# A graph layer's edge sum: a list's base is made behind a unit's second step, the product with it and the ranks one step later

## The chip, the cores and the metric

The kernel runs on one core of a Trainium2 chip. The metric is the device time of one execution in microseconds (us), lower is better. The kernel before has a median of 2552.46 us over 3 runs (2551.87 to 2553.11).

## What is computed

One layer of a graph network on 6250 nodes with 256 features, in float32. 200,000 edges, sorted by their target, carry a source, a target and a weight.

```python
xn = _layernorm(x, axis=-1)
gathered = values[:, None] * x[col]                    # one row per edge
out = jax.ops.segment_sum(gathered, row, num_segments=OUT_FEATURES) + bias
x = x + out_of_edges(xn, edge_index, edge_weight, node_vec1) + linear_attention(xn)
x = x + mixture_of_8_experts(_layernorm(x, axis=-1), top_k=2)
```

The change touches only the sum over the edges (the `gathered` and `segment_sum` lines above).

## The kernel before, in words

The program has five parts in a row: constants, `front` (layer norm, keys and values, loading the edges), `edge_sum`, `stragglers`, and the routing and the experts. All of the change is in `edge_sum`, which is written out without loops: four functions, one for each of TensorE (`tensor`), ScalarE (`scalar`), VectorE (`vector`) and GpSimd (`gpsimd`), each with its own instruction order, held together by semaphores.

The nodes are cut into 49 tiles of 128. The edges of a target tile are a list of 128 x 34 places. Each list is **sorted** by source tile (a *sort*, number `s`), so that later each (source tile, target tile) pair can be handled by small products. Independently the 49 x 7 pairs of target tile and group of seven source tiles are **summed**. Both kinds of work are interleaved by hand in `schedule`: eight sorts come first (`AHEAD`), then 7 groups of 7 *units*; a unit is 7 *steps*, one target tile each, so there are 343 steps. In the first six groups (42 units) each unit also does one sort, cut into pieces that hang behind its steps (`if more and i == 0:` and so on, where `i` is the step, 0 to 6; "the second step" is `i == 1`). The last group (7 units) has no sorts, but the second layer norm and the transposes for the routing.

A step of the sum, the same in each of the 343:

- VectorE: `picks` (L1295), `hots` (one-hot matrices: L1284, L1288) and `add` (L1316, adds a finished tile from PSUM to the sum in SBUF). `picks` runs one step ahead of TensorE's use, `hots` two, `add` one behind it.
- TensorE: `blocks` of the next tile (12 products, L903, waits for L1288), then `rows` of this one (4 products L911, 3 products L915; waits for ScalarE's copy and for the add of the tile two before).
- ScalarE: `evacuate` (L1027, copies the block matrices that L903 made).
- GpSimd: three gathers of rows from memory (L817).

The pieces of a sort in the order of the data: ScalarE repeats the list's tile numbers (`repeat_tiles`, L973) and fields (`repeat_fields`, L981); VectorE compares (`hot_tiles`, L1121); TensorE makes the **base** (`base`, L845: 34 products of 49 columns, which count for each partition how many edges of the same tile lie before it); ScalarE copies the base from PSUM (`take_base`, L989); VectorE multiplies it with the comparison (`rank_ahead`, L1134), compares within a row (`in_row`, L1125) and adds up the **ranks** (`rank`, L1140, L1142, L1145); ScalarE repeats the ranks (`repeat_ranks`, L996); VectorE makes `values` (L1164, four in all: two, one and one) and `slots` (L1153); TensorE makes the **table** from these (`make_table`, L854: 34 products of 196 columns); ScalarE unpacks it, and VectorE finishes it with `part` (L1172, L1173; in four of the seven units of a group) or `make_list` (L1180 to L1186; in the others).

Where the pieces stood before: step 0: TensorE `base` behind the rows, ScalarE unpacking, `take_base`, a repeat of the fields, VectorE the first two `values`; step 1: VectorE `part`, `in_row`, `rank_ahead`, ScalarE a repeat; step 2: VectorE `rank`; step 3: VectorE `make_list`, one of `values`; step 4: the last of `values`, ScalarE `repeat_ranks`; step 5: `slots`; step 6: `hot_tiles` for the next sort, TensorE `make_table`. Buffers of the sort are single: `values` may only be written again when the table that reads them is made (`table_made`).

Of the kernel before, what the change touches and what calls it, by code (L numbers as in the profile page):

```python
# [615 lines left out]
def edge_sum(nc, shared, edges, mixing, hot_w, xn_dram, xT_dram, base_dram, sum_dram, z_dram, Wg, bg, bias, wg, gb_row, G, NG, NT, N, D, HD):  # L616
# [22 lines left out]
    with ExitStack() as ctx:  # L639
# [86 lines left out]
        def later(s):  # L726

            return not (isinstance(s, int) and s == 0)
# [92 lines left out]
        def _(pe):  # L821
# [101 lines left out]
            def unit(g, k, odd, par, turn, more, after, q):  # L923
                t = g * NT + k * BU
                s = g * GRP + k + AHEAD
                pe.wait_ge(window_in[par], 16 * (turn + 1))
                for i in range(BU):
                    if i + 1 < BU:
                        blocks(t + i + 1, (i + 1) % 4, (odd + i + 1) % 2)
                    elif after:  # L930
                        blocks(t + BU, 0, 1 - odd)
                    rows(t + i, i, g * GRP + k, (odd + i) % 2, par)
                    if not more:
                        n = k * BU + i - BU - 1
                        if n >= 0:
                            turn_z(n)
                        if n >= 1:
                            logits(n - 1)
                    if more and i == 0:
                        base(s)  # L940
                    if more and i == 6:
                        make_table(s)
# [11 lines left out]
        def _(act):  # L954
# [29 lines left out]
            def take_base(s):  # L984

                if later(s):
                    act.wait_ge(ahead_done, 3 * s)
                act.wait_ge(base_done, s + 1)
                act.copy(base_sb[:, :], base_ps).then_inc(base_in, 1)  # L989
# [59 lines left out]
            def unit(g, k, odd, par, turn, more, after, q):  # L1049
                u = g * GRP + k  # L1050
                t = g * NT + k * BU
                s = u + AHEAD
                turned = isinstance(k, int) and k == GRP - 1
                for i in range(BU):
                    if i + 1 < BU:
                        evacuate(t + i + 1, (odd + i + 1) % 2)
                    elif after:
                        evacuate(t + BU, 1 - odd)
                    if not more:
                        if k > 0 and i == 0:  # L1060
                            root(k - 1)
                        if k * BU + i > BU:
                            take_z(k * BU + i - BU - 1)
                    if more and i == 0:
                        if odd == par:
                            unpack(s - 1, q, 1 - par)
                        else:
                            unpack_list(s - 1, lists_before(g + 1, q), q, 1 - par)
                        take_base(s)
                        repeat_fields(s, 2, 3)  # L1070
                    if more and i == 1:
                        repeat_fields(s, 3, FIELDS)
                    if after and i in (2, 4):
                        if turned:
                            act.wait_ge(unpacked, (g + 2) * GRP)
                            act.wait_ge(parted, (g + 2) * DENSE)
                            act.wait_ge(listed, (g + 2) * 3 * PICK)
                            take(t, 1 - odd, 1 - par, 0, i // 2 - 1)
                        else:
                            take(t, 1 - odd, par, k + 1, i // 2 - 1)  # L1080
                    if more and i == 3:
                        repeat_fields(s + 1, 0, 1)
                    if more and i == 4:
                        repeat_ranks(s)
                    if more and i == 5:
                        repeat_tiles(s + 1)
                    if more and i == 6:
                        repeat_fields(s + 1, 1, 2)
# [12 lines left out]
        def _(dve):  # L1101
# [206 lines left out]
            def unit(g, k, odd, par, turn, more, after, q):  # L1308
                u = g * GRP + k
                s = u + AHEAD  # L1310
                t = g * NT + k * BU

                def add(i):
                    row = acc[:, bass.ds(k * BU + i, 1), 0:D].rearrange("p a d -> p (a d)")
                    dve.wait_ge(o_done, t + i + 3)
                    dve.tensor_tensor(row, row, sum_ps[(odd + i) % 2], ALU.add).then_inc(o_added, 1)  # L1316

                    if not more:
                        dve.wait_ge(o_added, t + i + 3)
                        statistics(k * BU + i)  # L1320

                for i in range(BU):
                    if i + 1 < BU:
                        picks(t + i + 1, i + 1, odd)
                    elif after:
                        picks(t + BU, 0, 1 - odd)
                    if i == 2:
                        dve.wait_ge(cur_done, 2 * (u + 1))
                    if i + 2 < BU:
                        hots(t + i + 2, i + 2, odd, t + i + 2 if i + 2 < 3 else t + i + 1)  # L1330
                    elif after:
                        if i == BU - 2:
                            dve.wait_ge(cur_done, 2 * (u + 1) + 1)
                        hots(t + i + 2, i + 2 - BU, 1 - odd, t + i + 2)
                    if i > 0:
                        add(i - 1)
                    if not more and k > 0:
                        if i == 1:
                            reciprocals(k - 1)
                            normalize((k - 1) * BU)  # L1340
                        if i > 0:
                            normalize((k - 1) * BU + i)
                    if more and i == 0:
                        values(s, 0, 2)
                    if more and i == 1:
                        if odd == par:
                            part(s - 1, q, 1 - par)
                        in_row(s)
                        rank_ahead(s)
                    if more and i == 2:  # L1350
                        rank(s)
                    if more and i == 3:
                        if odd != par:
                            make_list(s - 1, lists_before(g + 1, q), q, 1 - par)
                        values(s, 2, 3)
                    if more and i == 4:
                        values(s, 3, FIELDS)
                    if more and i == 5:
                        slots(s)
                    if more and i == 6:  # L1360
                        hot_tiles(s + 1)
                add(BU - 1)
                if not more:
                    merge(k)
# [751 lines left out]
```

## Time and profile before, and how to read it

| what | value |
|---|---|
| median of 3 runs | 2552.46 us |
| span of the profiled execution, first to last instruction | 2536.7 us |
| its own time | not listed beside the span; the median is 15.8 us above the span |
| TensorE matmul busy | 2230.1 us, 88% of the span |
| VectorE busy | 1963.9 us, 77% |
| GpSimd busy | 1551.1 us, 61% |
| ScalarE busy | 1174.3 us, 46% |

PE is TensorE's matmuls, PEld its weight loads, DVE is VectorE, ACT ScalarE, POOL GpSimd. A number in brackets behind a row is the time that the engine sat idle before it, with what ended it: another engine's instruction, "issue" (nothing that the profile shows), or "remote" (a semaphore whose raiser the profile could not place near). The ends of matmuls are modelled, so a signal of PE is best read from when the engine that waits for it starts.

### The profile page before, as it was taken

How to read it: one execution, taken by the hardware profiler on the slowest of the kernel's cores; microseconds unless marked ns; L12 is line 12 of the kernel's file. 1: busy time of each engine (PE TensorE's matmuls, PEld its weight loads, DVE VectorE, ACT ScalarE, POOL GpSimd, SP SyncE). 2: the span in 40 equal slices, each digit the busy share in tenths (PEclk: the TensorE clock that was granted, in tenths of full speed). 3: DMA queues.
4: the chain of work that ended last, by engine and by line, in shares of the span. 5: the costliest groups of instructions: out<-in, count | busy, mean ns of one | idle time of the engine just before them, and what ended most of it. 6: DMA issues, size and time to landing. Idle time of an engine off the chain costs nothing. (4 is left out here: it accounts for less than half of the span.)

```text
span 2536.7 us, 45539 instructions
## 1 busy us (share of the span) xinstructions
PE 2230.1 (88%) x16549; PEld 1930.5 (76%) x16550; DVE 1963.9 (77%) x3350; ACT 1174.3 (46%) x1696; POOL 1551.1 (61%) x1356
## 2 busy tenths in 40 slices
PE   7987799999999899989988998999989944999993
PEld 4656687777887788778877787778877844999993
DVE  7989888788898788878877897879877757555552
ACT  2236544443444344434443454444322235888772
POOL 4750266666676566666665666666766612778883
PEclk9989999999999899989988999999999977999997
DMA  5532422222223222222222222222244453455555
GB/s 151 150 113 87 123 82 75 76 90 78 74 83 90 73 82 76 88 76 80 76 82 73 83 79 84 78 79 77 82 123 139 136 180 61 79 81 83 82 81 133
DMA packets 160931, 235.90 MB, mean 93 GB/s; under 512 B 54834, under 2 KB 121805, under 8 KB 160490
## 3 DMA queue, kind: packets, MB, share of 16 engines
q0 software_dynamic: 70896, 164.43, 25.4%
q1 hardware_dynamic: 75536, 55.29, 7.9%
q10 hardware_dynamic: 14314, 13.68, 1.6%
q8 instruction: 120, 1.97, 0.3%
q14 instruction: 65, 0.53, 0.1%
HBM read 186.46 MB, written 53.24 MB: 94 GB/s over the span
## 5 line engine op out<-in xcount | busy, mean ns | idle before, releaser
L817 POOL DMA_INDIRECT picked<-xn_dram,place x1029 | 1143.9, 1112 | 721.7 <-PE bank L915 289.8
L1027 ACT COPY stage<-bank 128x512 f32<-128x512 f32 x343 | 201.0, 586 | 796.9 <-remote 477.6
L915 PE MATMUL bank<-picked,pick_w 128*128 128x256 f32 x2058 | 518.4, 389 | 3.3 <-issue 3.3
L915 PEld LDWEIGHTS bank<-picked,pick_w 128*128 128x128 f32 x2058 | 405.7, 197 | 65.8 <-issue 5.2
L911 PE MATMUL bank<-window,stage 128*128 128x256 f32 x1568 | 416.9, 409 | 17.8 <-issue 12.8
L903 PE MATMUL bank<-hot_w,hots 128*128 128x128 bf16 x4116 | 312.0, 225 | 49.1 <-issue 44.8
L911 PEld LDWEIGHTS bank<-window,stage 128*128 128x128 f32 x1568 | 300.4, 202 | 65.1 <-issue 25.6
L1164 DVE TENSOR_TENSOR vals<-hot_t,field_rep 128x1666 bf16<-128x1666 bf16 x200 | 203.7, 1041 | 187.8 <-remote 180.2
L1288 DVE TENSOR_TENSOR hot_w<-hots,cur 128x1536 bf16<-128x1536 bf16 x343 | 328.6, 958 | 11.9
L903 PEld LDWEIGHTS bank<-hot_w,hots 128*128 128x128 bf16 x4116 | 267.1, 101 | 92.5 <-issue 54.5
L911 PE MATMUL bank<-stage 128*128 128x256 f32 x1176 | 315.5, 410 | 11.6 <-issue 10.4
L981 ACT COPY field_rep<-fields 128x1666 bf16<-128x1666 bf16 (+1 forms) x193 | 322.8, 1677 | 1.2 <-DVE vals L1164 1.2
L1284 DVE TENSOR_TENSOR hots<-ends,cur 128x1408 bf16<-128x1408 bf16 x343 | 303.1, 884 | 1.7 <-ACT cur L1021 1.7
L911 PEld LDWEIGHTS bank<-stage 128*128 128x128 f32 x1176 | 225.9, 203 | 49.0 <-issue 23.2
L1908 POOL DMA_INDIRECT sum_dram<-y,target x112 | 179.1, 1599 | 64.0 <-issue 31.1
L1316 DVE TENSOR_TENSOR acc<-acc,bank 128x256 f32<-128x256 f32 x343 | 142.3, 415 | 85.2 <-PE bank L915 44.7
L1295 DVE TENSOR_TENSOR pick_w<-hots,cur_w 128x384 f32<-128x384 bf16 x343 | 190.6, 556 | 0.2
L1899 POOL DMA_INDIRECT zin<-z_dram,token x112 | 115.5, 1031 | 83.4 <-POOLq L1600 49.6
L2002 PE MATMUL bank<-w,hh 128*128 x896 | 163.6, 282 | 1.1 <-DVE hl L2050 1.1
L854 PE MATMUL bank<-vals,slot 128*128 128x196 bf16 x1700 | 155.8, 249 | 4.9 <-issue 4.0
L854 PEld LDWEIGHTS bank<-vals,slot 128*128 128x128 bf16 x1700 | 147.9, 98 | 12.3 <-issue 5.8
L2002 PEld LDWEIGHTS bank<-w,hh 128*128 128x128 f32 x896 | 138.2, 189 | 1.4 <-issue 1.4
(253 smaller groups left out, 3414.6 us busy)
## 6 DMA issues: line engine op xcount, KB each, us to landing
picked<-xn_dram,place POOLq DMA_INDIRECT x1029
w<-in_L_ffn_W_dram SPq DMA_DIRECT2D x16, 512.0 KB, 8.9
xn_dram<-xn ACTq DMA_DIRECT2D x49, 128.0 KB, 1.9
xT_dram<-xT ACTq DMA_DIRECT2D x49, 128.0 KB, 2.1
base_dram<-acc SPq DMA_DIRECT2D x7, 896.0 KB
sum_dram<-acc SPq DMA_DIRECT2D x7, 896.0 KB
z_dram<-vals SPq DMA_DIRECT2D x7, 896.0 KB
out_dram<-sum_dram SPq DMA_DIRECT2D x1, 6250.0 KB, 21.8
```

Of the source, the lines that this page charges most:

```text
L817: pool.indirect_dma_start(out=picked[:, i % SETS * PICK + q, :], out_offset=None, in_=xn_dram, in_offset=bass.IndirectOffsetOnAxis(ap=plac ...
L854: mm = pe.matmul(table_ps, slot[:, c, :], vals[:, c, :, :], start=(c == 0), stop=(c == CH - 1))
L903: mm = pe.matmul(block_ps(pp, j), hot[buf][:, PICK + j, :], hot_w[buf][:, part, j, :], start=(part == 0), stop=(part == 2))
L911: pe.matmul(sum_ps[pp], block_sb[pp][:, j, :], window[par][:, j, :], start=(j == 0), stop=False)
L915: mm = pe.matmul(sum_ps[pp], pick_w[i % SETS][:, q, :], picked[:, i % SETS * PICK + q, :], start=False, stop=(q == PICK - 1))
L981: act.copy(field_rep[:, :, a:b, :], fields[:, a:b, bass.ds(s, 1), :].rearrange("p f a c -> p (a c) f").unsqueeze(3).broadcast_to([P, CH, b ...
L1027: act.copy(block_sb[pp].rearrange("p j c -> p (j c)"), banks[pp][:, :]).then_inc(a_copied, 1)
L1164: ins = dve.tensor_tensor(vals[:, :, f, :], hot_t[:, :, :], field_rep[:, :, f, :], ALU.mult)
L1284: dve.tensor_tensor(to[:, :, :].rearrange("p f (b r) -> p f b r", r=REP), ends[:, :, :].rearrange("p f (b r) -> p f b r", r=REP), of[:, i, ...
L1288: dve.tensor_tensor(hot_w[i % SETS][:, :, :, :].rearrange("p f g (b r) -> p f g b r", r=REP), to[:, AT_SRC:HOTS, :].rearrange("p g (b r) - ...
L1295: dve.tensor_tensor(pick_w[i % SETS][:, :, :].rearrange("p q (b r) -> p q b r", r=REP), hot[i % SETS][:, 0:PICK, :].rearrange("p q (b r) - ...
L2002: mm = pe.matmul(y_ps[i][:, n * D:(n + 1) * D], parts[a][:, c, n * P:(n + 1) * P], w, start=(m == 0), stop=(m == 3 * FC - 1))
```

## The change

Three places of the hand-written order. TensorE makes the base behind the rows of step 1, not of step 0. ScalarE takes it at step 1, behind the last repeat of the fields. VectorE multiplies with it at step 2 (before: step 1), and adds up the ranks at step 3 (before: step 2), ahead of `make_list` and one of `values`. No instruction is added or removed. The eight sorts ahead of the units are not touched.

```diff
@@ TensorE, unit
-                    if more and i == 0:
+                    if more and i == 1:
                         base(s)
@@ ScalarE, unit
                             unpack_list(s - 1, lists_before(g + 1, q), q, 1 - par)
-                        take_base(s)
                         repeat_fields(s, 2, 3)
                     if more and i == 1:
                         repeat_fields(s, 3, FIELDS)
+                        take_base(s)
@@ VectorE, unit
                         in_row(s)
+                    if more and i == 2:
                         rank_ahead(s)
-                    if more and i == 2:
+                    if more and i == 3:
                         rank(s)
-                    if more and i == 3:
                         if odd != par:
                             make_list(s - 1, lists_before(g + 1, q), q, 1 - par)
                         values(s, 2, 3)
```

TensorE around the first unit's base, of before (`bank` is any PSUM bank; L903 is the next tile's blocks, L911 and L915 this tile's rows):

```order
 L915 MATMUL bank<-picked,pick_w 128x256 x3
 L845 MATMUL bank<-hot_t,before 128x49 x34
 L903 MATMUL bank<-hot_w,hots 128x128 x12
 L911 MATMUL bank<-window,stage 128x256 x4
 L915 MATMUL bank<-picked,pick_w 128x256 x3
```

and of the change:

```order
 L903 MATMUL bank<-hot_w,hots 128x128 x12
 L911 MATMUL bank<-window,stage 128x256 x4
 L915 MATMUL bank<-picked,pick_w 128x256 x3
 L845 MATMUL bank<-hot_t,before 128x49 x34
 L903 MATMUL bank<-hot_w,hots 128x128 x12
```

The base has moved past one whole step of the sum (12, 4 and 3 products).

VectorE, steps 1 to 3 of a unit, of before (`earlier` is what `rank_ahead` and `rank` write, `same` what `in_row` writes):

```order
 L1125 TENSOR_TENSOR same<-tile_pad,tile_rep 128x1156
 L1134 TENSOR_TENSOR earlier<-hot_t,base_sb 128x34x49
 L1295 TENSOR_TENSOR pick_w<-hots,cur_w 128x384
 L1284 TENSOR_TENSOR hots<-ends,cur 128x1408
 L1288 TENSOR_TENSOR hot_w<-hots,cur 128x1536
 L1316 TENSOR_TENSOR acc<-acc,bank 128x256
 L1140 TENSOR_TENSOR earlier<-earlier,same 128x34x34
 L1142 TENSOR_TENSOR earlier<-earlier 128x34x24
 L1145 TENSOR_REDUCE rank<-earlier 128x34
```

and of the change:

```order
 L1125 TENSOR_TENSOR same<-tile_pad,tile_rep 128x1156
 L1295 TENSOR_TENSOR pick_w<-hots,cur_w 128x384
 L1284 TENSOR_TENSOR hots<-ends,cur 128x1408
 L1288 TENSOR_TENSOR hot_w<-hots,cur 128x1536
 L1316 TENSOR_TENSOR acc<-acc,bank 128x256
 L1134 TENSOR_TENSOR earlier<-hot_t,base_sb 128x34x49
```

The product with the base now stands behind the next step's add instead of ahead of that step; the three rank instructions follow one step after it. On ScalarE `take_base` (L989) changes places with one repeat (L981) and an evacuation (L1027) and now stands right behind the second repeat.

## Rows read from the trace of the kernel before

**Rows 1.** The page's first line.

```profile
span 2536.7 us, 45539 instructions
```

**Rows 2.** Busy time by stretch: 41 of the 42 units with a sort, then the first without.

```profile
core 0: us, PE busy (x) PEld busy (x) DVE busy (x) ACT busy (x) POOL busy (x), PEclk, DMA share, GB/s
334.00:1803.00 1469.00, 1346.11 (x10252) 1163.16 (x10251) 1218.99 (x1777) 649.14 (x838) 956.18 (x862) 0.93 0.27 80
1803.00:1834.00 31.00, 29.41 (x218) 25.91 (x217) 28.50 (x41) 8.28 (x11) 23.85 (x21) 1.00 0.30 86
```

**Rows 3.** Waits in 334 to 1803: who waited for whom, us, times, longest.

```profile
DVE vals L1164 <- remote: 180.2, 37, 8.3
...
PE bank L845 <- issue: 61.2, 83, 1.2
...
PE bank L903 <- DVE hot_w L1288: 1.1, 1, 1.1
```

**Rows 4.** Timeline of one unit, steps 6 to 3, PE, ACT and DVE: start, us, instruction.

```profile
979.42 3.06 PE L854 MATMUL bank<-vals,slot 128*128 128x196 bf16 x34
...
986.06 0.24 PE L845 MATMUL bank<-hot_t,before 128*128 128x49 bf16 x3
...
987.17 2.00 DVE L1164 TENSOR_TENSOR vals<-hot_t,field_rep 128x1666 bf16<-128x1666 bf16 x2 [4.87 <-remote]
...
989.89 0.99 PE L845 MATMUL bank<-hot_t,before 128*128 128x49 bf16 x22 [1.15 <-issue]
...
991.35 0.41 DVE L1316 TENSOR_TENSOR acc<-acc,bank 128x256 f32<-128x256 f32 x1
991.68 0.77 DVE L1125 TENSOR_TENSOR same<-tile_pad,tile_rep 128x1156 bf16<-128x1156 bf16 x1
...
993.15 0.20 ACT L989 CAST base_sb<-bank 128x49 bf16<-128x49 f32 x1 [2.16 <-remote]
...
993.39 1.05 DVE L1134 TENSOR_TENSOR earlier<-hot_t,base_sb 128x1666 bf16<-128x1666 bf16 x1 [0.93 <-ACT base_sb L989]
994.35 0.55 DVE L1295 TENSOR_TENSOR pick_w<-hots,cur_w 128x384 f32<-128x384 bf16 x1
994.50 1.46 PE L915 MATMUL bank<-picked,pick_w 128*128 128x256 f32 x6
...
995.74 0.96 DVE L1288 TENSOR_TENSOR hot_w<-hots,cur 128x1536 bf16<-128x1536 bf16 x1
...
996.62 0.41 DVE L1316 TENSOR_TENSOR acc<-acc,bank 128x256 f32<-128x256 f32 x1
...
999.35 0.55 DVE L1295 TENSOR_TENSOR pick_w<-hots,cur_w 128x384 f32<-128x384 bf16 x1
```

**Rows 5.** The same unit, its steps 3 to 5: the list and TensorE's need of VectorE.

```profile
1001.94 0.27 DVE L1180 TENSOR_SCALAR table<-table 128x49 uint16<-128x49 uint16 x1
...
1002.63 1.04 DVE L1164 TENSOR_TENSOR vals<-hot_t,field_rep 128x1666 bf16<-128x1666 bf16 x1
...
1004.97 0.96 DVE L1288 TENSOR_TENSOR hot_w<-hots,cur 128x1536 bf16<-128x1536 bf16 x1
...
1007.03 0.83 PE L903 MATMUL bank<-hot_w,hots 128*128 128x128 bf16 x12
```

**Rows 6.** Timeline of an earlier unit: a base without gaps and its copy.

```profile
601.58 1.04 PE L845 MATMUL bank<-hot_t,before 128*128 128x49 bf16 x34
...
602.79 0.20 ACT L989 CAST base_sb<-bank 128x49 bf16<-128x49 f32 x1 [3.10 <-PE bank L845]
```

**Rows 7.** Timeline of the last unit with a sort: end of its base and the copy.

```profile
1782.60 1.12 PE L845 MATMUL bank<-hot_t,before 128*128 128x49 bf16 x23 [1.16 <-issue]
...
1785.93 0.20 ACT L989 CAST base_sb<-bank 128x49 bf16<-128x49 f32 x1 [1.73 <-remote]
```

**Rows 8.** Busy time by stretch in one unit's first step; columns as in rows 2.

```profile
1020.80:1024.20 3.40, 1.23 (x13) 0.66 (x11) 2.01 (x3) 0.00 (x0) 2.72 (x2) 1.00 0.27 78
1024.20:1027.60 3.40, 2.89 (x38) 2.71 (x38) 3.36 (x7) 1.53 (x2) 1.89 (x2) 0.50 0.27 74
```

## The prediction

> **What bounds the kernel now.** I read the page first for the span, 2536.7 us [rows 1]; the median of the runs, 2552.5, lies 15.8 above it. Then the busy time by stretch. 41 of the 42 units that the change touches fill 1469 us, 35.8 each [rows 2]. In them the matmuls are busy 1346 us and VectorE 1219, 92% and 83%, so TensorE bounds and VectorE follows closely. The table of waits says how closely: TensorE's L903 waited for VectorE's L1288 once in 41 units, for 1.1 us [rows 3]. So there is slack between them, but I have to measure it, since the change pushes work of VectorE into a later step.
>
> What keeps a unit at 35.8 us shows in the timeline of one [rows 4]. The table's matmuls run from 979.42 to 982.48. VectorE waits for exactly that and gets it at 987.17, 4.7 us late, after 4.87 us of "remote" idling. The same wait is 180.2 us over 37 units [rows 3]. TensorE has meanwhile issued the next step and three matmuls of the base, and then it halts: the base that takes 1.04 us elsewhere [rows 6] stretches from 986.06 to 990.88, in pieces. So behind each table there is a stretch in which TensorE's signals come late and then its issue stops. The reader should see two things in it: the base of before stands in that stretch, and the "issue" idling ahead of its matmuls adds up to 61.2 us [rows 3]. What causes the stretch no row says. The first unit without a sort still begins with a table but has no base, and there TensorE idles only 31.0 - 29.4 = 1.6 us [rows 2] against (1469 - 1346) / 41 = 3.0.
>
> The other late signal is the base's own. In the unit shown its last matmul ends at 990.88 and ScalarE copies it at 993.15, 2.3 us later [rows 4]; in the last unit 1783.72 and 1785.93, 2.2 [rows 7]; but in another 602.62 and 602.79, 0.2 [rows 6]. Over the timeline of all 42 units, 27 are late by 1.5 us or more and 15 prompt or nearly so.
>
> **The change part by part.**
>
> *TensorE.* The same 34 matmuls, one step later, 42 times; their own time is about 0.9 us (34 in 1.04 with the tail of the last, [rows 6]) in either place. Taken alone this is 0. Where the halt falls on the base now, it will fall on the next L903 and rows. Price 0, if the halt is set by something before the base; its ends are -61 us (all of L845's idling goes and nothing else idles) and +61 (the base takes a second halt in its new place as long as the one it leaves behind). I take 0, since the lateness has begun with the table, 6.6 us before the first base matmul is issued.
>
> One thing differs inside the halt's tail: after the halt the granted clock is 0.50 (1.2 GHz) for 3.4 us, following 3.4 us in which TensorE was busy 1.23 [rows 8]. The base's 22 matmuls in that time took (0.99 - 0.18) / 21 = 38 ns each against 26 ns, losing 0.3 us. Rows in that microsecond would lose half of it, 0.5. That is 0.2 us more in some 24 units, +4 us at most, inside the range. The Trainium skill (TensorE: Matmul & The Clock Gate, Part 1) says that no small matmul starts sooner than about 25 ns after the one before, and that the array falls to half rate after idling. By that rule the base is the cheapest thing to have in a half-rate stretch, which speaks against the change by these same few us; the trace agrees on both counts, with 26 ns and 0.50.
>
> *ScalarE.* `take_base` is one copy of 0.20 us [rows 4]. Queued behind it now is the evacuation of step 2's next blocks, which TensorE only makes after the base anyway. Its cover is TensorE's own order: 0. The repeat of the fields and one evacuation are freed from waiting for it, which nobody waits for: 0.
>
> *VectorE.* Until L1288 of step 4 the same instructions run before and after, in another order, so their sum cannot make it late; only idling inserted between them can. I lay one unit [rows 4, 5] out anew. Before: add at 991.35, `in_row`, 0.93 of idling, product at 993.39, picks and hots 2.27 (994.35 to 996.62), add, ranks 2.40 (to 999.35), later the list 0.69 (1001.94 to 1002.63). L1288 of step 4 is done at 1005.93, and TensorE needs it at 1007.03 [rows 5]: a margin of 1.1. After: `in_row` to 992.37, picks and hots to 994.64. TensorE's rows of step 1 end 0.9 earlier, since the base isn't ahead of them, at 995.1 instead of 995.96; add to 995.4. Now VectorE is at the product and has to wait for the base, whose matmuls run from 995.1 to 996.0. With a prompt signal the product starts at 996.3, with the late one at 998.4. Then product 0.96, picks and hots 2.27, add 0.33, ranks 2.40, list 0.69, values 0.95, picks and hots 2.27, together 9.87: L1288 is done at 1006.2 or 1008.3. The first has a margin of 0.8, the second makes TensorE wait 1.3. In a unit without a list it is 0.7 less: 0.6. So **a prompt base costs 0, a late one 1.3 (18 units have a list) or 0.6 (24 have none), 0.9 on average.** With the base ahead of `in_row` this was covered; this wait is what the change adds. Behind step 4 nothing more is lost: `slots` are needed only by the table, and the two `values` of the next step 0 wait for the late table anyway.
>
> *How often late.* 27 of 42 before. The new place is one step further from the table, where signals recover: the rows of step 1 end at 995.96 and their add starts at 996.62, straight behind VectorE's own work, so that signal was less than 0.7 late [rows 4]. But the base is itself late in units where the halt lay ahead of it. Ends 0 and 42 units; I take a quarter, 10, nearer to the prompt end. **Sum: 10 x 0.9 = +9 us on the span, 2545.7, and with the 15.8 around it 2561.5.**
>
> **The rivals.**
>
> 1. *The halt shrinks* (faster). The table and the base are two bursts of 34 short products; before, one step of the sum lay between them, now two. If the base feeds the halt, half of L845's 61.2 us could go: -31, 2522; a third is -20. For it: the unit with a table and no base, 1.6 against 3.0 us of idling [rows 2]; also VectorE's 0.93 of idling for the base goes in units where it now has other work. Against: in the unit shown the lateness precedes the base, and one unit is little evidence. It decides from 0.33 us less halt per unit on: 9 us of my forecast and 5 more, over 42.
>
> 2. *Nothing moves* (same). The base is prompt in its new place, and the halt takes the next instructions instead: 0 to 5 us, 2552 to 2557. For it: behind the table TensorE issued one step, 26 matmuls, and 3 of the base, and then halted [rows 4]; with a base one step later it would issue as many of the next step. The Trainium skill (TensorE: Matmul & The Clock Gate, the table at its head) gives TensorE a queue of 64 instructions; if a full queue is what stops it, the halt comes as many instructions behind the table, whichever they are. The 29 matmuls with as many weight loads fit that, though nothing here shows the queue.
>
> 3. *Every base is late* (slower than forecast). 42 x 0.9 = +38: 2590. For it: 27 of 42 are late now. Against: the add of the second step is not held up.
>
> **How the numbers follow.** Forecast of some late bases 0.30, all or most of them late 0.15, nothing moves 0.22, the halt shrinks 0.33. Within 0.2%, 5 us, a measurement of this kernel cannot tell a difference. Faster is rival 1, 0.33; same is rival 2, 0.22; slower is the forecast and rival 3, 0.45. The range goes from 2520, half of L845's idling gone, to 2590, all bases late. Below it lie halts that vanish, above it a second halt, together 0.2. The forecast's own range is 2556 to 2575.
>
> **What would show each step.** Right: in the after trace the waits of L903 (and its weight loads) for L1288 grow from 1.1 us to some 9, most in units with a list, and L1134 idles for `base_sb` in most units, for 0.9 us where the base is prompt and 3 where late. The 180 us that `vals` idles should stay, and L845's 61 us of issue idling turn up ahead of L903, L911 and L915. Wrong: if `vals` idles clearly less, or the 42 units take less than 35.8 us each, the halt depends on the base (rival 1). If L903 doesn't wait for L1288, VectorE's slack was larger than I worked out, or its signal prompt (rival 2).

## The result, and the profile after

The change makes the kernel slower: 2600.98 us (median of 4 runs, 2598.70 to 2605.76) against 2552.16 us before in the same set (4 runs). The ratio is 1.0275, 95% interval 1.0231 to 1.0319. The forecast of 2561.5 had the direction, and the time lies above its range. It is even above rival 3 (every base late, 2590).

The page's first lines after:

```profile
span 2597.0 us, 45539 instructions
## 1 busy us (share of the span) xinstructions
PE 2239.3 (86%) x16549; PEld 1922.0 (74%) x16550; DVE 1963.6 (76%) x3350; ACT 1171.5 (45%) x1696; POOL 1530.6 (59%) x1356
```

The span grew by 60.3 us [rows 1], and no engine has more work. This run's own time is 2598.85, 1.9 above its span. So of the 15.8 us that the prediction put around the span of before, some 2 can be overhead; the rest is the distance between one execution and the median of the others.

The stretch of the same 41 units as in [rows 2] is now 1524 us, not 1469:

```profile
core 0: us, PE busy (x) PEld busy (x) DVE busy (x) ACT busy (x) POOL busy (x), PEclk, DMA share, GB/s
335.00:1859.00 1524.00, 1354.54 (x10238) 1154.12 (x10237) 1219.84 (x1776) 645.64 (x838) 933.91 (x861) 0.94 0.27 77
```

VectorE's work is the same to a microsecond; TensorE has 8 us more busy time and 47 more of idling. The waits of that stretch, to be held against [rows 3]:

```profile
engine line waited for: us in total, times, longest us
ACT base_sb L989 <- remote: 183.1, 39, 6.3
...
DVE vals L1164 <- remote: 122.1, 41, 5.9
DVE earlier L1134 <- ACT base_sb L989: 120.1, 36, 5.0
PE bank L903 <- issue: 77.1, 124, 1.7
PE bank L911 <- issue: 38.5, 41, 1.8
PE bank L903 <- DVE hot_w L1288: 37.2, 39, 2.5
...
PE bank L911 <- ACT stage L1027: 14.0, 10, 1.8
```

Three things are to be seen. L903 waits for L1288 in nearly every unit, 37.2 us where it was 1.1. L1134 idles for the base in nearly every unit. And L845's 61.2 us of issue idling have gone from the list, while L903 and L911 have more. Over the whole kernel the issue idling ahead of L845, L903 and L911 was 61.2 + 44.8 + 23.2 = 129.2 us before, and after it is 0 + 92.7 + 39.8 = 132.5. Between these two kernels the halt is as long as it was and has moved.

One unit shows the mechanism. Timeline, steps 1 and 2, TensorE, ScalarE and VectorE:

```profile
1023.43 2.74 PE L915 MATMUL bank<-picked,pick_w 128*128 128x256 f32 x6
...
1025.99 1.06 PE L845 MATMUL bank<-hot_t,before 128*128 128x49 bf16 x34
...
1026.21 0.42 DVE L1316 TENSOR_TENSOR acc<-acc,bank 128x256 f32<-128x256 f32 x1 [2.19 <-PE bank L915]
...
1026.89 0.83 PE L903 MATMUL bank<-hot_w,hots 128*128 128x128 bf16 x12
...
1029.37 0.20 ACT L989 CAST base_sb<-bank 128x49 bf16<-128x49 f32 x1 [5.63 <-remote]
1029.60 1.05 DVE L1134 TENSOR_TENSOR earlier<-hot_t,base_sb 128x1666 bf16<-128x1666 bf16 x1 [2.97 <-ACT base_sb L989]
...
1030.64 0.83 PE L903 MATMUL bank<-hot_w,hots 128*128 128x128 bf16 x12
1030.85 0.58 ACT L1027 COPY stage<-bank 128x512 f32<-128x512 f32 x1 [1.28 <-remote]
...
1031.49 1.99 PE L911 MATMUL bank<-window,stage 128*128 128x256 f32 x8
```

The rows ahead of the base signal promptly: they end at 1026.17 and the add starts at 1026.21. The base's 34 matmuls follow without a gap, are through at 1027.05 by the record, and their copy starts at 1029.37. By the record the base takes 1.04 to 1.06. From its first matmul to the copy it is 3.3 to 3.4 us in 29 of the 42 units, 5.4 or 5.5 in 10, 4.1 in one, and less in two (1.3 and 2.6).

Where the time of a unit went, as the mean distance of the same matmul (the last L915) from one step to the next, us; the right column is the sum:

| kernel | 0-1 | 1-2 | 2-3 | 3-4 | 4-5 | 5-6 | 6-0 | unit |
|---|---|---|---|---|---|---|---|---|
| before | 7.40 | 3.92 | 3.75 | 3.79 | 3.75 | 3.75 | 9.35 | 35.7 |
| after | 8.00 | 4.88 | 4.03 | 3.75 | 4.88 | 3.75 | 7.88 | 37.2 |

The step from 6 to 0 and that from 0 to 1 hold the table and the halt: 16.75 before, 15.88 after, less by 0.87, and the base's 0.86 of issue is no longer in it. Step 1 to 2 has the base now, +0.96. Step 2 to 3 has +0.28, and step 4 to 5, where VectorE is late, +1.13. The two last make 42 x 1.41 = 59 us, nearly all of the 60.3.

### The profile page after: what moved, and what is told of

It is laid out like the page before. It is cut to its first block and busy times, and to the rows that moved or that the text cites. A ratio compares the mean times of both kernels' runs of the same rounds, so it can differ in the third digit from the quotient of the medians.

```text
span 2597.0 us, 45539 instructions
## 1 busy us (share of the span) xinstructions
PE 2239.3 (86%) x16549; PEld 1922.0 (74%) x16550; DVE 1963.6 (76%) x3350; ACT 1171.5 (45%) x1696; POOL 1530.6 (59%) x1356
## 5 line engine op out<-in xcount | busy, mean ns | idle before, releaser
L817 POOL DMA_INDIRECT picked<-xn_dram,place x1029 | 1122.5, 1091 | 802.7 <-PE bank L915 377.5
L1027 ACT COPY stage<-bank 128x512 f32<-128x512 f32 x343 | 201.4, 587 | 793.2 <-PE bank L903 564.7
L915 PE MATMUL bank<-picked,pick_w 128*128 128x256 f32 x2058 | 523.3, 392 | 0.4 <-issue 0.3
L915 PEld LDWEIGHTS bank<-picked,pick_w 128*128 128x128 f32 x2058 | 411.4, 200 | 63.7 <-issue 1.0
L911 PE MATMUL bank<-window,stage 128*128 128x256 f32 x1568 | 422.2, 416 | 30.2 <-issue 21.2
L903 PE MATMUL bank<-hot_w,hots 128*128 128x128 bf16 x4116 | 314.8, 220 | 134.5 <-issue 92.7
L903 PEld LDWEIGHTS bank<-hot_w,hots 128*128 128x128 bf16 x4116 | 256.8, 99 | 188.7 <-issue 106.3
L911 PEld LDWEIGHTS bank<-window,stage 128*128 128x128 f32 x1568 | 305.5, 205 | 82.6 <-issue 32.8
L911 PE MATMUL bank<-stage 128*128 128x256 f32 x1176 | 316.3, 415 | 27.1 <-issue 18.6
L1288 DVE TENSOR_TENSOR hot_w<-hots,cur 128x1536 bf16<-128x1536 bf16 x343 | 328.6, 958 | 11.9
L981 ACT COPY field_rep<-fields 128x1666 bf16<-128x1666 bf16 (+1 forms) x193 | 331.0, 1719 | 1.2 <-DVE vals L1164 1.2
L1164 DVE TENSOR_TENSOR vals<-hot_t,field_rep 128x1666 bf16<-128x1666 bf16 x200 | 203.6, 1041 | 122.5 <-remote 122.1
L911 PEld LDWEIGHTS bank<-stage 128*128 128x128 f32 x1176 | 227.2, 204 | 72.2 <-issue 31.3
L1134 DVE TENSOR_TENSOR earlier<-hot_t,base_sb 128x1666 bf16<-128x1666 bf16 x50 | 52.4, 1048 | 135.9 <-ACT base_sb L989 123.9
```

Source lines behind the costliest of these rows:

```text
L817: pool.indirect_dma_start(out=picked[:, i % SETS * PICK + q, :], out_offset=None, in_=xn_dram, in_offset=bass.IndirectOffsetOnAxis(ap=plac ...
L903: mm = pe.matmul(block_ps(pp, j), hot[buf][:, PICK + j, :], hot_w[buf][:, part, j, :], start=(part == 0), stop=(part == 2))
L911: pe.matmul(sum_ps[pp], block_sb[pp][:, j, :], window[par][:, j, :], start=(j == 0), stop=False)
L915: mm = pe.matmul(sum_ps[pp], pick_w[i % SETS][:, q, :], picked[:, i % SETS * PICK + q, :], start=False, stop=(q == PICK - 1))
L981: act.copy(field_rep[:, :, a:b, :], fields[:, a:b, bass.ds(s, 1), :].rearrange("p f a c -> p (a c) f").unsqueeze(3).broadcast_to([P, CH, b ...
L1027: act.copy(block_sb[pp].rearrange("p j c -> p (j c)"), banks[pp][:, :]).then_inc(a_copied, 1)
```

## The experiments

Twelve kernels in fourteen runs (e13 and e14 are e4 and e1 once more). "The kernel before" is timed beside each set; its median moves from set to set (2529 to 2552), so ratios are what to compare. L903, L1134 and so on name the same instructions in all of them, also where an edit moved the lines. In the quoted texts W is the theory that VectorE's wait at the product is the loss.

The same steps as in the table above for five of them, us. The first column is step 6 to 0 and 0 to 1 together, with the base's 0.86 taken off where it stands in there (before, e1 and e4):

| kernel | 6 to 1, no base | 1-2 | 2-3 | 3-4 | 4-5 | unit |
|---|---|---|---|---|---|---|
| before | 15.9 | 3.92 | 3.75 | 3.79 | 3.75 | 35.7 |
| after | 15.9 | 4.88 | 4.03 | 3.75 | 4.88 | 37.2 |
| e1 | 15.2 | 4.04 | 3.75 | 3.75 | 4.00 | 35.4 |
| e2 | 15.0 | 4.96 | 4.30 | 3.75 | 4.07 | 35.8 |
| e4 | 14.1 | 4.04 | 3.77 | 3.96 | 4.44 | 34.9 |
| e7 | 14.4 | 4.91 | 4.08 | 4.02 | 6.95 | 38.1 |

**e1: TensorE's base back at step 0, ScalarE and VectorE as in the change.**

```diff
-                    if more and i == 1:
+                    if more and i == 0:
                         base(s)
```

> The changed kernel with TensorE's base put back behind the rows of step 0; ScalarE's copy stays at step 1, VectorE's product at step 2, the ranks at step 3. Theory W (VectorE waits for a base that is signalled late, and so comes late with the one-hot matrices of step 4): the base is made one step before it is wanted, so the wait of 3 us per unit at L1134 goes and with it TensorE's waits for L1288; 2545 to 2560 us, as the kernel before. Theory C (ranks, list and values crowded into step 3 make VectorE late by themselves): the crowding is still there, 2590 to 2605. Theory H (the halt behind the table grew because something else stands in it): 2550 to 2560 too, but then with L1134's wait unchanged in size.

Measured: 2509.91 us, ratio 0.9854 (0.9786 to 0.9923). L903's wait for L1288 is 8.6 us. The same kernel again (e14) had 0.9938.

> The same kernel as e1. If it is faster than the kernel before as e1's runs had it: ratio 0.979 to 0.992. If e1's four runs were a chance: 0.995 to 1.005.

e14: 2517.04 us, 0.9895 to 0.9981. The later product and ranks do no harm and even gain 0.6 to 1.5%. The loss needs the base's new place. TensorE's order is that of before here, and still steps 6 to 1 take 0.7 us less a unit (0.5 in e14), so how long TensorE halts also depends on what the other engines do.

**e2: the product at step 3, ahead of the ranks; the base stays behind step 1.**

```diff
-                    if more and i == 2:
-                        rank_ahead(s)
                     if more and i == 3:
+                        rank_ahead(s)
                         rank(s)
```

> The changed kernel with VectorE's product with the base moved on to step 3, right ahead of the ranks; base and its copy stay at step 1. Crowds step 3 still more (by 1.0 us), but VectorE meets the base some 3.7 us later. Theory W: L1134 no longer idles, L903 no longer waits for L1288; what is left is ScalarE's copy, which waits for the base ahead of an evacuation that TensorE wants (some 0.3 us per unit, 14 us): 2555 to 2570. Theory C: worse than the changed kernel, 2610 to 2640. Theory H: unchanged, 2595 to 2605.

Measured: 2535.93 us, ratio 1.0002 (0.9963 to 1.0041). The base is still late in 30 of 42 units (by over 1.5 us), yet the time is that of before, and the wait is gone. Waits of e2, units:

```profile
PE bank L903 <- issue: 61.1, 90, 1.1
...
PE bank L903 <- DVE hot_w L1288: 12.6, 22, 1.8
PE bank L911 <- ACT stage L1027: 11.8, 13, 1.8
```

L1134 stands in the list no longer. So the loss hangs on VectorE standing at L1134, as the prediction had it, and not on TensorE's base by itself. Only part of it is recovered where the prediction put it: step 4 to 5 falls by 0.81, to 4.07, or 34 us in 42 units. Steps 6 to 1 fall by 0.93, or 39 us, with TensorE's order unchanged, and 2 to 3 grows by 0.27. Why the halt is shorter when VectorE doesn't stand, no run shows. What is left, L911's wait, is taken up with e7.

**e7 and e3: ScalarE's copy of the base behind the evacuation of step 2's next blocks**, e7 on the change, e3 on e2.

```diff
                         repeat_fields(s, 3, FIELDS)
+                    if more and i == 2:
                         take_base(s)
```

> The changed kernel with ScalarE's copy of the base moved on behind the evacuation of step 2, and nothing else. Theory W: TensorE's waits for the evacuation (16.7 us in all) go, but VectorE's product comes later by the evacuation's time where it waits, 0.6 us in most units, and TensorE waits for it at step 5: 2600 to 2620. If ScalarE's wait had been the main cost: 2560 to 2580.

Measured: e7 2642.65 us, ratio 1.0387 (1.0331 to 1.0442). The copy comes 4.27 us behind the base's last matmul, not 2.32, and step 4 to 5 grows by 2.07 us, to 6.95. So 1.95 us more of lateness cost 2.07 in the step where TensorE needs VectorE. But a unit is only 0.9 us longer (42 us in the median of the runs), since steps 6 to 1 take 1.49 less: where TensorE waits longer for VectorE, its halt is shorter. Waits of e7, units (L1289 is L1288):

```profile
PE bank L903 <- DVE hot_w L1289: 93.1, 66, 2.7
...
PE bank L911 <- ACT stage L1027: 18.0, 34, 1.8
```

The second row is no measure of ScalarE's queue behind the base: 26 of its 34 waits, and all ten of the change's 14.0 us, lie between steps 0 and 1, in the halt. Step 2 to 3 is the measure. With the copy behind the evacuation it is 4.08, and 4.03 in the change, so L911 was not held up by `take_base`. The timeline above says by what: the evacuation at 1030.85 had ScalarE idle for 1.28 us ahead of it, with L903 through at 1027.72 by the record. L903 signals late too, behind a base, and L911 starts at 1031.49, 0.06 behind the end of the evacuation.

> As the last one, and ScalarE's copy of the base is moved on behind the evacuation of step 2. Theory W with the second, smaller wait (ScalarE held by the late base ahead of an evacuation): another 5 to 14 us less, 2545 to 2560; the waits of TensorE for L1027 fall back to about 3 us from 35. If that wait costs nothing: no difference from the last one. Theory H: 2595 to 2605.

Measured: e3 2582.23 us, 1.0153 (1.0095 to 1.0211), where e2 had 1.0002. Unexpected: steps 0 to 5 are as in e2, but step 6 to 0 takes 10.72 us on average (9.04 in e2), 13.3 in half of the units. Nothing waits for another engine there; the issue idling grows. I have no cause for it.

**e4: the base spread**, five matmuls behind each of the seven products of the rows of step 1 (L911 and L915), all else as in the change.

```diff
+                    part = (lambda n: base_part(s, n)) if more and i == 1 else None
-                    rows(t + i, i, g * GRP + k, (odd + i) % 2, par)
+                    rows(t + i, i, g * GRP + k, (odd + i) % 2, par, part)
...
-                    if more and i == 1:
-                        base(s)
```

> The changed kernel with the base's 34 matmuls spread over the rows of step 1, five behind each of the seven products, not in one burst behind them; VectorE and ScalarE as changed. Theory B (a burst of short matmuls is what makes the signal late, by 2.4 us for the base and 4.4 for the table): the base's signal is prompt, L1134 waits 0 to 1 us instead of 3, 2555 to 2570. If the lateness belongs to the place behind the table and not to the burst: as the changed kernel, 2590 to 2605.

Measured: 2502.93 us, ratio 0.9869 (0.9802 to 0.9936). Timeline of one unit, base, copy and product (L853, L1004 and L1149 here):

```profile
1018.94 0.26 PE L853 MATMUL bank<-hot_t,before 128*128 128x49 bf16 x4
1019.05 0.83 PE L912 MATMUL bank<-hot_w,hots 128*128 128x128 bf16 x12
...
1019.30 0.20 ACT L1004 CAST base_sb<-bank 128x49 bf16<-128x49 f32 x1 [2.11 <-PE bank L853]
...
1019.54 1.05 DVE L1149 TENSOR_TENSOR earlier<-hot_t,base_sb 128x1666 bf16<-128x1666 bf16 x1
```

The copy starts 0.09 us behind the last matmul in the median, and in 7 of 42 units over 1.5. The place is the same as in the change, so it takes the burst to make the signal late. The kernel run again (e13):

> The same kernel as e4. If it is faster than the kernel before as e4's runs had it: ratio 0.980 to 0.994. If e4's four runs were a chance: 0.995 to 1.005.

e13: 2504.58 us, ratio 0.9887 (0.9842 to 0.9931). It beats both kernels. A unit is 0.8 us shorter than before: steps 6 to 1 take 1.8 less, steps 3 to 5 take 0.9 more.

**e9: two bursts of 17**, one ahead of the rows of step 1, one behind.

```diff
+                    if more and i == 1:
+                        base_half(s, 0)
                     rows(t + i, i, g * GRP + k, (odd + i) % 2, par)
...
                     if more and i == 1:
-                        base(s)
+                        base_half(s, 1)
```

> The change with the base in two bursts of 17, one ahead of the rows of step 1, one behind them. Theory B (the signal comes late because the burst itself is worked off slower than it is issued, by about 2.3 us / 34 = 0.07 us for each matmul, and the rows between let it catch up): the copy of the base starts 1.2 us behind the last base matmul instead of 2.3, L1134 waits for it about 1.1 us less in each unit (124 us falls to some 75), L903 waits for L1288 some 12 us instead of 40, and the time is near 2560. Rival H (the signal is late because the step before holds a halt or because of where the base stands, whatever its length): the lateness stays at 2.3 and the time at 2600.

Measured: 2535.29 us, ratio 0.9993 (0.9957 to 1.0029). L1134 idles 18.7 us for `base_sb`, L903 2.8 us for L1288. The lateness is 0.18 us in the median and not the 1.2 I expected: half of the matmuls leave not half of the lateness, but next to none. So the lateness isn't proportional to the burst.

**e10: the base twice**, its 34 matmuls issued two times in a row (the second pass begins the sum anew).

```diff
-                for c in range(CH):
+                for c in [c for r in range(times) for c in range(CH)]:
```

> The change with the base's 34 matmuls of the units issued twice in a row into the same bank; the second pass begins the sum anew, so the value is the same. Its issue alone adds 0.86 us x 42 = 36 us. Theory B (burst): the lateness doubles from 2.3 to some 4.6 us behind the last matmul, so the product starts 3.2 us later in each unit, L903's wait for L1288 takes nearly all of it, and the time is 2600 + 42 x 3.2 = 2734. Rival H: the lateness stays at 2.3, and the time is 2600 + 36 = 2636.

Measured: 2746.85 us, ratio 1.0843 (1.0792 to 1.0894). The total agrees with the burst theory's 2734, its way doesn't. L903 hardly waits for L1288 (7.4 us). TensorE itself is held up, in the middle of the burst:

```profile
1002.96 1.40 PE L845 MATMUL bank<-hot_t,before 128*128 128x49 bf16 x48
...
1004.60 0.33 PE L845 MATMUL bank<-hot_t,before 128*128 128x49 bf16 x6 [0.24 <-issue]
1005.34 0.28 PE L845 MATMUL bank<-hot_t,before 128*128 128x49 bf16 x4 [0.41 <-issue]
1006.05 0.32 PE L845 MATMUL bank<-hot_t,before 128*128 128x49 bf16 x6 [0.44 <-issue]
...
1008.54 0.20 ACT L989 CAST base_sb<-bank 128x49 bf16<-128x49 f32 x1 [6.38 <-PE bank L845]
```

48 matmuls are issued 26 ns apart, and from then on some five in 0.7 us. From the first matmul to the copy it is 5.6 us. A unit is 40.70 - 37.18 = 3.5 us longer, 0.10 us for each of the 34 added matmuls, not the 0.026 at which they are issued. This is at least their cost, as VectorE's lateness is hidden behind it now: step 1 to 2, where they stand, is 4.9 us longer, 0.145 for each.

**e11: the table twice**, on the kernel before, by the same edit in `make_table`, in the units.

> The kernel before with the table's 34 matmuls of the units issued twice in a row. Their issue adds 3.06 us x 42 = 129 us: 2681 if nothing else changes. Theory B (a burst is worked off slower than it is issued, and the halt is TensorE's issue being stopped until that is made up for): the wait of vals for the table grows by more than the 3.06 us in each unit (180 us to over 400 in all), the issue idling of TensorE behind it, 129 us, doubles to 250 or more, and the time is 2780 to 2850. Rival P (the halt is something that comes once in a unit by itself, since it does so in the units without a sort too): issue idling stays near 129 us and the time is 2680.

Measured: 2743.70 us, ratio 1.0814 (1.0762 to 1.0866). The halt stands inside the table now:

```profile
1030.20 3.64 PE L854 MATMUL bank<-vals,slot 128*128 128x196 bf16 x40
...
1034.86 0.50 PE L854 MATMUL bank<-vals,slot 128*128 128x196 bf16 x4 [1.02 <-issue]
...
1036.27 0.81 PE L854 MATMUL bank<-vals,slot 128*128 128x196 bf16 x4 [0.91 <-issue]
...
1043.42 2.00 DVE L1164 TENSOR_TENSOR vals<-hot_t,field_rep 128x1666 bf16<-128x1666 bf16 x2 [8.38 <-PE bank L854]
```

Units are 40.92 - 35.70 = 5.2 us longer in the profiled execution, the slowest of the four; by the medians of the times it is (2743.70 - 2536.08) / 42 = 4.9. So an added matmul costs 0.145 to 0.153 us, and the records of the table have them 0.09 apart (3.06 for 34). The added halt is some 2 us a unit, so the time is less than the 2780 to 2850 I expected, and clearly more than rival P's 2680. The gaps of TensorE in the 42 units, all lines together, grow from 120 to 165 us. The base behind step 0 has no gap here, and its copy comes 3.3 us behind its first matmul in all 42 units:

```profile
1006.54 1.04 PE L845 MATMUL bank<-hot_t,before 128*128 128x49 bf16 x34
...
1009.82 0.20 ACT L989 CAST base_sb<-bank 128x49 bf16<-128x49 f32 x1 [7.03 <-remote]
```

**e5: the base spread over the rows of step 0, on the kernel before; e8: the same with ScalarE's and VectorE's order of the change.**

> The kernel before (base in step 0, product in step 1, ranks in step 2) with the base's 34 matmuls spread over the rows of step 0, five behind each of the seven products. Theory B (the burst makes the signal late): the copy of the base starts within 0.5 us of its last matmul in most units, and as nothing is crowded the time is at or below that of the changed kernel with the base spread, 2485 to 2510 us. If the halt behind the table stretches whatever stands there: the base's signal is late in half of the units as before, 2525 to 2550.

Measured: e5 2550.24 us, ratio 1.0015 (0.9970 to 1.0060). The copy is 0.09 us behind the last matmul in the median, over 1.5 in 15 units, and the time gains nothing by it. Step 0 to 1 falls from 7.40 to 3.95, and step 6 to 0 grows from 9.35 to 12.79: together 16.75 before, 16.74 here. The halt is not shortened by taking the burst away behind it; it comes earlier by as much.

> ScalarE's and VectorE's order of the change, TensorE's base five matmuls at a time between the seven products of rows of step 0. It joins what was faster in two runs: a base with a prompt signal (2503) and a base early enough for the product one step later (2510). If the two add up: both waits, of L1134 for the base and of L903 for L1288, are near nothing, and the time is 2490 to 2500. If each only took away the same wait of VectorE: 2505. Rival: it goes as the same spreading in the kernel before (2550, the halt falls on the step ahead of it instead).

Measured: e8 2525.07 us, ratio 0.9951 (0.9915 to 0.9986). The two gains don't add up: it lies above the 2490 to 2505 expected for that, and below the rival's 2550.

**e6 and e12: the table apart.** e6 spreads it over the rows of the next unit's step 0, e12 makes it in two bursts of 17 with 12 blocks between; the base in both as in e4.

> The changed kernel with the base spread over the rows of step 1 and the table's 34 matmuls, too, spread over the rows of the next unit's step 0, five behind each of the seven products. Theory B extended (the burst of the table is what makes its signal late and then halts TensorE, 4 to 5 us per unit): the halts shrink or go, 2400 to 2460 us. If the halt comes from the number of instructions in the unit or from something else that returns once per unit: it stays, 2490 to 2530.

Measured: e6 2543.54 us, ratio 1.0005 (0.9975 to 1.0035). Both forecasts are missed. The table is ready a step later, and VectorE with it: step 4 to 5 is 5.72. Waits of e6 (L922 is L903, L1313 is L1288):

```profile
DVE vals L1189 <- remote: 225.5, 40, 6.9
...
PE bank L922 <- DVE hot_w L1313: 72.8, 43, 4.5
```

> The base spread over the rows of step 1 as in e4, and the table's 34 matmuls in two bursts of 17, the first behind step 6, the second one step's 12 blocks later, ahead of the rows of the next unit's step 0. Theory R (a unit stands on TensorE's real rate, which its issue only runs ahead of: by the doubled bursts 0.10 us for each matmul of the base and 0.15 for each of the table, so 26.3 + 3.5 + 5.0 = 34.8 us a unit, and e4 has 34.9): nothing to gain, 2495 to 2515, and the halts move about. Rival S (the halt is the price of one long burst, as the base's late signal was): issue idling of TensorE in the units falls to under half, the units take 33 us each, and the time is near 2430.

Measured: e12 2523.80 us, ratio 0.9952 (0.9919 to 0.9984), units of 35.3 us, gaps of TensorE 105 us where e4 has 99. Rival S (33 us a unit, 2430) falls. Theory R isn't refuted, but the time is somewhat above its 2495 to 2515.

## Why the prediction was wrong

*TensorE, priced 0: right in the sum.* The halt moved and kept its length: 129.2 us of issue idling became 132.5, and the two steps that hold it lost 0.87 us, the base's own issue. e5 shows the same from the other side, and rival 1 fell by this. In part it was luck. That "the halt is set by something before the base" is too simple: with TensorE's order unchanged, steps 6 to 1 are 0.7 us shorter in e1 than before and 0.9 shorter in e2 than in the change. Against e1, the change pays 0.5 to 0.7 us a unit in the halt too, which the sum had at nothing.

*VectorE's price: right.* A late base was to cost 1.3 us with a list and 0.6 without, 0.9 on average; step 4 to 5 grew by 1.27 and 0.58 in the medians and 1.13 in the mean. e2, where the product is one step later, has most of this gone. It is the price in that step; e7 shows that the unit pays less than the step.

***How often late*: this step failed.** It took 10 of 42 units, since "the new place is one step further from the table, where signals recover". The base is late in 41. I had taken the lateness for something that the base inherits from the halt, and the prompt add ahead of the product for the sign that it had passed. That add is prompt indeed (1026.17 to 1026.21 above), and the base behind it is late all the same: the lateness arises in the base. Half bursts (e9) and the spread base (e4) in the same place are prompt, late by over 1.5 us in 6 and in 7 of 42 units. The rows of before could have said so. Of its 42 bases 17 have no gap in them, and only 6 of these 17 are as prompt as the one in [rows 6], 7 are at 3.3 us, the others between. I had that one case in the rows and took it for the rule. Rival 3's "against" was the same error. The count of before was also a little high: 25 of the 42 are late by 1.5 us or more, and the other two of its 27 by 1.37 and 1.49.

*ScalarE, priced 0: its queue rightly, the wait missed.* "TensorE only makes after the base anyway" holds for the issue of the blocks. But their signal is late as well, so the evacuation is late and L911 waits for it. In 37 of the 42 units L911 of that step starts within 0.12 us of the evacuation's end, and its distance from the last L903 is 0.23 us in the median, where it was 0.06. Pauses this short stand in no row of the waits. Step 2 to 3 grew by 0.28, 12 us in all. e7 shows that the place of `take_base` in ScalarE's queue isn't the cause.

*"Their own time is about 0.9 us" in either place:* right for the issue, too small as a price. In the doubled bursts an added matmul costs 0.10 us (base) and 0.15 (table), stops of the issue included.

*`vals` idles as long (180 us): wrong.* It idles 122.1. The larger part of that is VectorE, late by then: on average over the units it reaches the wait 4.8 us behind the table's first matmul, where it was 3.9. The rest is the table's signal: L1164 starts 7.8 us behind that matmul, where it was 8.5. It was a sign for rival 1 in my list; the first part has nothing to do with it, and the halt behind the table is no shorter for the second.

*The Trainium skill's 25 ns* (TensorE: Matmul & The Clock Gate, Part 1) is a distance of issue. The records agree, with 26 ns in [rows 6]. As the price of an added matmul it is too low by a factor of four: e10 has 0.10 us.

*Rival 2's queue* of 64 instructions (the same page, the table at its head) is neither shown nor refuted: e10 issues 48 matmuls with as many weight loads, 96 instructions, before its first gap, but how many of them were done by then no row says. In 37 of its 42 units the first gap comes after 36 to 67 matmuls of the base, and behind a table it comes 37 to 99 matmuls from the table's first in the kernel before, 36 to 68 in the change. So the halt isn't a fixed number of instructions behind the table.

*The sum.* With 42 units late the prediction's own working gives 2590 by rival 3. Added 12 for L911, it is 2602; measured 2601. The 15.8 us around the span are in the first of these and for the most part not real, so some of this agreement is luck: from span to span it is 38 + 12 = 50 against 60.

What stays open. First, why a burst makes TensorE late in the units at all. It doesn't do so by itself. The eight sorts ahead of the units have the same 34 matmuls at the same distance, and their copy comes 1.13 to 1.14 us behind the first one in six of them. Timeline of the change, the last of the eight:

```profile
279.05 1.13 PE L864 MATMUL bank<-hots,picked 128*128 128x256 f32 x4 [1.28 <-DVE acc L1190]
...
280.01 1.04 PE L845 MATMUL bank<-hot_t,before 128*128 128x49 bf16 x34
281.15 0.20 ACT L989 CAST base_sb<-bank 128x49 bf16<-128x49 f32 x1 [3.12 <-PE bank L845]
```

There TensorE has pauses (39.0 of 50 us busy in the stretch around it); in the units it has next to none ahead of the burst. That is the difference I see; I haven't tested it. Second, what the units stand on. By the doubled bursts a unit has 7 x 3.75 + 34 x 0.10 + 34 x 0.15 = 34.8 us of TensorE's time, and the best kernel, e4, has 34.9. That would make the halt a debt of issuing too fast, with little left to gain from reordering; e7, where waiting for VectorE shortens the halt, fits it. Against it speak e12's 35.3 and e3's longer halt without more work, and with e10's 0.145 for the base the sum is 36.3, more than e4 takes. The kernel before had 0.8 us more a unit than e4, which I can't put down to one wait.

## What to carry to other kernels

A run of some 30 short matmuls (34 here) in a TensorE that never pauses may signal 2 us after its record ends, and so may what is issued next; take its length from its first matmul to the moment that an idle waiting engine starts, over all its occurrences. Don't put the consumer of such a burst one step behind it in the order of an engine with little slack: give it another step (e2, a ratio of 1.0002 to the kernel before where the change has 1.0275) or spread the burst between long matmuls (e4, 1.1 to 1.3% less than before).

When a row's lateness has two readings (inherited, or its own), look for the case in which the instruction ahead is prompt. And price a wait by the whole unit, not by the step in which it falls: in e7 the step grew by 2.07 us and the unit by 0.9.

## What the runs showed of the hardware

The lateness comes in steps. From the first matmul of a base without gaps to its copy it is 1.2, 1.9, 2.6, 3.3, 4.1 or 5.4 us (before and after together, 59 bases, each within 0.15), so 1.2 and a whole number of 0.7 us more, mostly three of them. The gaps of the halts have the same step: e10's matmuls above go on at 1004.60, 1005.34, 1006.05, 0.7 us apart. I had expected a lateness in proportion to the work.

The clock is granted in full while the lateness builds up, and falls behind the halt. Busy time by stretch in the unit of the change shown above: its table and step 0, the halt, the rows of step 0, and the base:

```profile
1008.80:1015.40 6.60, 6.60 (x61) 6.15 (x61) 5.12 (x8) 0.00 (x0) 4.90 (x6) 1.00 0.35 102
1015.40:1019.80 4.40, 1.47 (x15) 0.88 (x13) 3.35 (x5) 0.58 (x3) 2.77 (x3) 0.93 0.31 89
1019.80:1025.50 5.70, 5.64 (x13) 4.54 (x14) 4.18 (x6) 3.94 (x6) 2.63 (x3) 0.50 0.24 69
1025.50:1029.10 3.60, 3.60 (x55) 3.10 (x54) 0.42 (x1) 0.00 (x0) 2.05 (x3) 0.93 0.15 41
```

The third column from the end is the granted clock: 1.00 (2.4 GHz), 0.93, then 0.50 (1.2 GHz) for the 5.7 us behind the halt, in which eight L911 take 3.78 us where they take 1.95 in the next step. The low part of the last row lies ahead of the base. From its first matmul to its copy the clock is granted in full:

```profile
1025.99:1029.37 3.38, 3.38 (x56) 3.17 (x55) 0.42 (x1) 0.00 (x1) 2.32 (x3) 1.00 0.17 47
```

So it is in all 42 units of the change (0.99 the lowest), so a low clock under the base isn't what makes it late. What the clock did just ahead of it goes with the size. Of the 29 bases at 3.3 to 3.4 us, 28 have a lower clock in the 2 us before their first matmul; of the ten at 5.4 or 5.5, none has. No run tests why.
